# Deformable-convolution block: projections one turn later, one corner instruction, and a product behind every outer product and every addition

## The reference, cut to what matters

```python
# x: (4, 32, 32, 128); G = 8 groups of 16 channels, P = 9 points per pixel and group
xp = gn(x) @ in_w + in_b                          # what is sampled
x1 = silu(batchnorm(depthwise_conv3x3(gn(x))))
offset = x1 @ off_w + off_b                       # (x, y) shift of each point
mask = softmax(x1 @ mask_w + mask_b over the 9 points)
samples = bilinear_sample(xp padded by 1, grid + offset)   # four corners per point
out = (samples * mask).sum(over points) @ out_w + out_b
x = x + out
t = x + attention(layernorm(x));   y = t + experts(layernorm(t))
```

## Time and profile before

| | us |
|---|---|
| median of 3 runs | 665.65 (665.49 to 667.91) |
| the profiled execution's own time | 666.92 |
| its span, first to last instruction | 665.1 |
| PE busy over the span | 599.5 (90%) |
| DVE busy over the span | 550.3 (83%) |
| ACT busy over the span | 234.6 (35%) |
| POOL busy over the span | 320.1 (48%) |

### The profile page before, as it was taken

The page is one execution under the profiler, slowest core; times in us unless marked ns, Lnnn a source line. Parts: engine busy times, 40 slices in busy tenths (PEclk is TensorE's granted clock), DMA queues, the critical chain, the costliest instruction groups (busy, mean ns, idle before and its releaser), DMA issues.

```text
span 665.1 us, 11013 instructions
## 1 busy us (share of the span) xinstructions
PE 599.5 (90%) x3618; PEld 442.4 (67%) x3618; DVE 550.3 (83%) x1030; ACT 234.6 (35%) x351; POOL 320.1 (48%) x408
## 2 busy tenths in 40 slices
PE   5989979979989989889797789999999999979995
PEld 4466656657567667566575567777777777775774
DVE  4668998999999999999999989847767666655877
ACT  6063503405307107126144000344544544415331
POOL 7605775786688578748588810202222211115222
PEclk9789989989989989989997999999999999999999
DMA  7097402103003007000000000000000000004111
GB/s 182 20 337 234 164 0 70 46 3 112 1 3 113 1 1 277 4 1 2 1 1 5 0 1 1 0 2 0 1 1 1 1 1 0 1 6 124 48 33 48
DMA packets 26242, 30.75 MB, mean 46 GB/s; under 512 B 5572, under 2 KB 18324, under 8 KB 26196
## 3 DMA queue, kind: packets, MB, share of 16 engines
q1 hardware_dynamic: 24094, 29.77, 13.8%
q0 software_dynamic: 1408, 0.36, 0.5%
q10 hardware_dynamic: 694, 0.01, 0.1%
HBM read 25.07 MB, written 5.05 MB: 45 GB/s over the span
## 4 chain that ended last, share of the span: by engine, by line
PE 57%; DVE 28%; issue 10%; ACT 2%; DMA 1%; SPq 1%; DVEq 0%; POOL 0%; ACTq 0%; POOLq 0%
DVE prod L1657 13%; PE banks L935 11%; PE banks L1062 9%; PE pair L1042 8%; DVE outer L1589 5%; PE pair L1130 4%; PE banks L1052 4%; PE pair L865 4%; PE banks L1168 4%; PE pair L857 2%; DVE stencil L1598 2%; PE banks L922 2%; PE banks L957 2%; DVE hats L1540 2%; DMA res<-in_x_dram 1%
## 5 line engine op out<-in xcount | busy, mean ns | idle before, releaser
L935 PE MATMUL banks<-ident,prod 128*128 128x128 f32 x1440 | 203.6, 282 | 35.2 <-DVE prod L1657 34.0
L935 PEld LDWEIGHTS banks<-ident,prod 128*128 128x128 f32 x1440 | 165.5, 143 | 91.4 <-DVE prod L1657 64.3
L1657 DVE TENSOR_TENSOR prod<-shifted,stencil 128x1024 f32<-128x1024 f32 (+1 forms) x208 | 218.3, 1084 | 5.2 <-ACT stencil L601 3.5
L1413 POOL TENSOR_TENSOR rstd_now<-mv_now,neg_half 128x2 f32<-128x2 f32 x32 | 22.9, 716 | 124.1 <-DVE mv_now L1705 124.1
L865 PE MATMUL pair<-xg,dw_diag 128*128 128x512 f32 x144 | 74.3, 618 | 1.4 <-DVE xg L1467 1.4
L1308 POOL DMA_INDIRECT got<-padded,cell_now x44 | 57.8, 1314 | 19.0 <-issue 10.1
L1062 PEld LDWEIGHTS banks<-shifted 128*128 128x128 f32 x512 | 60.2, 192 | 8.1 <-issue 6.1
L1062 PE MATMUL banks<-shifted 128*128 128x128 f32 x512 | 63.3, 277 | 2.4 <-ACT shifted L741 1.4
L1589 DVE TENSOR_TENSOR outer<-hats 128x800 f32<-128x800 f32 x56 | 55.8, 996 | 6.1 <-PE banks L922 6.1
L1042 PE MATMUL pair<-shifted 128*128 128x512 f32 x128 | 60.6, 596 | 0.1
L1720 DVE TENSOR_REDUCE neg_max<-pair 128x1 f32<-128x1024 f32 x32 | 39.2, 1225 | 23.1 <-PE pair L1042 22.0
(11 more groups left out here) (264 smaller groups left out, 957.6 us busy)
## 6 DMA issues: line engine op xcount, KB each, us to landing
shifted<-padded SPq DMA_DIRECT2D x42, 256.0 KB
shifted<-padded SPq DMA_DIRECT2D x14, 640.0 KB
res<-in_x_dram SPq DMA_DIRECT2D x4, 512.0 KB, 6.4
padded<-stage SPq DMA_DIRECT2D x4, 512.0 KB, 10.2
stage<-in_L_ffn_W_dram SPq DMA_DIRECT2D x16, 128.0 KB, 2.2
out_dram<-res SPq DMA_DIRECT2D x16, 128.0 KB, 1.8
got<-padded,cell_now POOLq DMA_INDIRECT x44, 2.8
padded<-stencil SPq DMA_DIRECT2D x2, 228.0 KB, 2.6
```

What stands on the lines that cost most here:

```text
L935: mm = pe.matmul(acc_of(c, r), prod[:, slot, r * G:(r + 1) * G, :].rearrange("p g c -> p (g c)"), ident[:, :], is_transpose=True, start=(t ...
L1657: ins = ve.tensor_tensor(prod[:, dx:dx + n, :, :], shifted[:, dx:dx + n, bass.ds(((c % HALF) * ROWS + dy) * G, ROWS * G), :], stencil_of[: ...
```

## The change

Four things are changed together. The products are dealt out differently: one unit between every outer product and its addition, one behind every addition, instead of none or one between and one or two behind. The two corner instructions, of 64 results each, become one of 128 (`outermost` gives the addresses). `project` of chunk k-2 runs in turn k at taps 17, 19, 21, 23, where `project` of chunk k-1 ran at 35 to 41; chunks 5 and 6 are projected between the last chunk's taps, so that only the last chunk is left for the start of the attention. ACT's and DVE's order and waits follow: `residual` moves behind the far counts, `copy_sums` of the last chunk ahead of `residual` of chunk 5, and the last `residual_rest` ahead of the second softmax of the attention.

```diff
-AT_CONV, AT_FAR, AT_OFFSETS, AT_SAMPLES, AT_PROJECT = 4, 15, 30, 31, 35
+AT_CONV, AT_FAR, AT_PROJECT, AT_OFFSETS, AT_SAMPLES = 4, 15, 17, 30, 31
+LAST_PROJECT, LAST_SAMPLES = 8, 20
-POINT_FILL = (1, 0, 1, 0, 1, 0, 1, 0, 0)
-STENCIL_FILL = (0, 2, 1, 2, 1, 2, 1, 2, 2)
+POINT_FILL = (1, 1, 1, 1, 1, 1, 1, 1, 1)
+STENCIL_FILL = (0, 1, 1, 1, 1, 1, 1, 1, 1)
...
+        def outermost(axis, per_column, per_row):
+            first = hats[:, axis, :, :].rearrange("p (g q) t -> p g (q t)", q=PTS)[:, :, 0:1]
+            return bass.AP(tensor=first.tensor, offset=first.offset,
+                           ap=[first.ap[0], first.ap[1], [per_column, 2], [per_row, 2]])
...
                 prepare(j + 2, sums_at=3)
                 clear_stencil(j)
-                if not isinstance(j, int) or j > 0:
-                    residual(j - 1)
                 signs_of(j + 2)
                 if conv_ahead:
                     silu(j + 3)
                 count_out(j + 2)
+                if not isinstance(j, int) or j > 0:
+                    residual(j - 1)
                 copy_out(j)
...
-            residual(CHUNKS - 3)
             copy_sums(CHUNKS - 1)
+            residual(CHUNKS - 3)
             copy_out(CHUNKS - 2)
+            residual(CHUNKS - 2)
             copy_out(CHUNKS - 1)
...
             copy_keys(2)
-            residual_rest(CHUNKS - 2)
             copy_keys(3)
             copy_normed(4)
             exps(0, 0)
+            residual_rest(CHUNKS - 1)
             copy_normed(5)
             copy_keys(4)
             exps(1, 1)
-            residual_rest(CHUNKS - 1)
             copy_keys(5)
...
+                    if t == 0 and c >= 2:
+                        pe.wait_ge(samp_t_done, c - 1)
...
-                    if 0 <= n < B and between == 0 and not first:
-                        project(k - 1, n, n + 1, conv_out if n == B - 1 else None)
+                    if 0 <= n < B and between == 0 and k >= 2:
+                        project(k - 2, n, n + 1, conv_out if n == B - 1 else None)
...
-            add_up(CHUNKS - 1, first_of(BEGIN), AT_SAMPLES)
-            add_fix(CHUNKS - 2)
-            add_up(CHUNKS - 1, AT_SAMPLES, NEAR)
+            for i in range(first_of(BEGIN), NEAR):
+                if i == LAST_SAMPLES:
+                    add_fix(CHUNKS - 2)
+                for k, at in ((CHUNKS - 3, LAST_PROJECT), (CHUNKS - 2, LAST_SAMPLES + 8)):
+                    n, between = divmod(i - at, 2)
+                    if 0 <= n < B and between == 0:
+                        project(k, n, n + 1, conv_out if n == B - 1 else None)
+                add_up(CHUNKS - 1, i, i + 1)
             add_fix(CHUNKS - 1)
-            project(CHUNKS - 2, 0, 1, conv_first)
             project(CHUNKS - 1, 0, 1, conv_first)
...
-            project_rest(CHUNKS - 2, 1)
...
-            project_rest(CHUNKS - 1, 2)
-            project_rest(CHUNKS - 1, 3)
...
-                for kx in range(2):
-                    x0, y0 = (2 * 3 * TAPS + TAPS - 1) * kx, 2 * 3 * TAPS * kx
-                    last = ve.scalar_tensor_tensor(at_corner[:, :, kx, :], at[:, 0, :, x0:x0 + 2 * TAPS + 1:2 * TAPS], 0.0,
-                                                   at[:, 1, :, y0:y0 + 3 * TAPS:2 * TAPS + TAPS - 1], ALU.is_le, ALU.is_lt)
+                last = ve.tensor_tensor(at_corner[:, :, :, :], outermost(0, 2 * 3 * TAPS + TAPS - 1, 2 * TAPS),
+                                        outermost(1, 2 * 3 * TAPS, 2 * TAPS + TAPS - 1), ALU.logical_and)
```

More of the change, by code:

```diff
@@ L707, in _ @@
             copy_sums(CHUNKS - 1)
+            residual(CHUNKS - 3)
             copy_out(CHUNKS - 2)
+            residual(CHUNKS - 2)
             copy_out(CHUNKS - 1)
-            for i, k in enumerate((CHUNKS - 2, CHUNKS - 1)):
-                sc.wait_ge(conv_first, i + 1)
-                residual_of(k, 0, 1)
+            sc.wait_ge(conv_first, 1)
+            residual_of(CHUNKS - 1, 0, 1)
             def copy_normed(j):
@@ L949, in project @@
                 pe.wait_ge(res1_done, CHUNKS - 1 if last else k + 1)
-                if n0 > 0 and done is not None and n1 - n0 > 1:
-                    pe.wait_ge(res1_first, 2 if last else 1)
                 for n in range(n0, n1):
@@ L1081, in attend, with project_rest @@
                     keys(p + LEAD)
-            def project_rest(k, n):
+            def project_rest(n):
                 if n == 1:
-                    pe.wait_ge(res1_first, k - CHUNKS + 3)
-                project(k, n, n + 1, conv_out if n == B - 1 else None)
+                    pe.wait_ge(res1_first, 1)
+                project(CHUNKS - 1, n, n + 1, conv_out if n == B - 1 else None)
             normed_to_t(0)
-            pe.wait_ge(samp_t_done, CHUNKS)
-            project_rest(CHUNKS - 2, 1)
             normed_to_t(1)
             keys(0)
-            project_rest(CHUNKS - 2, 2)
+            project_rest(1)
             normed_to_t(2)
             keys(1)
-            project_rest(CHUNKS - 2, 3)
+            project_rest(2)
             normed_to_t(3)
@@ L1103, in _ @@
             normed_to_t(4)
-            project_rest(CHUNKS - 1, 1)
+            project_rest(3)
             pe.wait_ge(keyed_done, TILES // 2)
@@ L1546, in corners @@
                     ve.sem_inc(dve_waited, 1)
-                at = hats[:, :, :, :].rearrange("p a (g q) t -> p a g (q t)", q=PTS)
-                for kx in range(2):
-                    x0, y0 = (2 * 3 * TAPS + TAPS - 1) * kx, 2 * 3 * TAPS * kx
-                    last = ve.scalar_tensor_tensor(at_corner[:, :, kx, :], at[:, 0, :, x0:x0 + 2 * TAPS + 1:2 * TAPS], 0.0,
-                                                   at[:, 1, :, y0:y0 + 3 * TAPS:2 * TAPS + TAPS - 1], ALU.is_le, ALU.is_lt)
+                last = ve.tensor_tensor(at_corner[:, :, :, :], outermost(0, 2 * 3 * TAPS + TAPS - 1, 2 * TAPS),
+                                        outermost(1, 2 * 3 * TAPS, 2 * TAPS + TAPS - 1), ALU.logical_and)
                 last.then_inc(corners_done, 1)
@@ L1763, in _ @@
                     if j + 1 == TILES // 2 - 1:
-                        ve.wait_ge(res1_first, 2)
+                        ve.wait_ge(res1_first, 1)
+                        ve.wait_ge(res1_done, CHUNKS)
                     token_stats(j + 1, 2 * ((j + 1) % 2), var1)
```

## The result

The changed kernel takes 681.53 us (median of five, 677.95 to 693.01), the kernel before 665.49 us beside it; the ratio is 1.023, interval 1.020 to 1.027. The profiled execution, 693.01 us, is the longest of the five, so the sizes read from it are those of a long one; the kinds of waits are what counts.

A forecast was written before the change was run, and what follows sets the result against it. DVE, 96% busy in turns 0 to 6, was taken to set a turn's length. Terms 7.5 + 2.0 + 0.3 - 1.4 + 1.0 = 9.4 us gave 656.3 us against 665.65, range 653 to 661.2, chance 0.50.

The forecast's parts named there:

- The pauses: On DVE, the 0.11 us between each outer product and its addition goes, 35 times over seven turns, 3.85 us.
- The gaps stay: Rival: DVE still pays the 0.11 us even behind a product; 1.6 us less gain, 657.9 us, chance 0.05.
- the rule on the DRAIN: Skill page: DVE's pipeline empties behind every instruction before the next starts, so the 0.11 us would stay.
- PE's clock no longer falls: Rival: projections fill PE's idle stretch, so its clock stays at 1.00; 2.8 us more gain, 653.5 us, chance 0.18.
- the forecast's terms for turns 0 to 5: Gain 7.5 us: 1.55 a turn in turns 1 to 4, 0.76 in turn 0, about 0.5 in turn 5.
- The new waits for `copy_sums`: DVE, earlier than the chain through PE and ACT, would still wait in turns 1 to 4; 0.61 us in turn 3.
- The first half of a turn: Gaps and corner save 2.6 us; new waits of 0.46 us before outer product 3 cost 2.3; net gain 0.3.
- Turn 6: DVE's wait of 1.70 us before the last chunk goes, plus 0.33 of gaps: gain 2.0 us.
- the last chunk: Eight projections between its taps make DVE's products wait for PE: loss 1.4 us, bounds 0.5 and 6.3.
- the attention: At its start, an earlier residual and two projections fewer in PE's queue bring the scores about 1.0 us earlier.
- the second lump: Last chunk: the later group of four projections over seven taps, said to hold DVE 0.9 us.
- PE has no room: Rival: projections hold outer products 3 to 5 and the last chunk's products; 18.4 us lost, 674.7 us, chance 0.05.

The follow-up runs named there:

- gaps_back: The changed kernel with the two fill tables of before, so the 0.11 us pause between outer product and addition returns: 664.85 us, ratio 0.999.
- no_far_points: The changed kernel with POOL's work on the listed far points left out, the sum staying zero: 652.50 us, ratio 0.981.

## Why the prediction was wrong, point by point

**The step that failed** is the first: "DVE sets the length of a turn, and its idle time and its instruction order are what can be shortened there." For the turns the sum followed DVE, PE and ACT and had no POOL in it, so POOL's chain was put at nothing without a reason, though `add_fix` stands in PE's queue at tap 31 and waits for POOL. No rival spoke of it either. In the changed kernel PE waited there for 35.5 us and DVE's outer products behind it for 41.8; without POOL's work the same kernel takes 652.50 us. The profile of before had two warnings. POOL's lists, in turns of 47.5 us, came 57.5 us apart:
```profile
165.87 0.55 POOL L1386 CAST far_list_i<-far_list 1x8 int32 x1 [2.06 <-issue]
...
223.38 0.95 POOL L1386 CAST far_list_i<-far_list 1x8 int32 x1 [2.21 <-issue]
...
280.89 1.05 POOL L1386 CAST far_list_i<-far_list 1x8 int32 x1 [2.21 <-ACT far_counts L670]
```
and the margin at which PE took its sum shrank from turn to turn: 49.1 us in turn 1, then 29.8, 19.8, and 9.9 in turn 4. There the sum of chunk 3 was done at 277.94 + 0.73 = 278.67, and PE took it at 288.54:
```profile
277.94 0.73 POOL L1353 TENSOR_TENSOR stage<-stage,got_sum 128x16 f32 x1 [0.42 <-POOL got_sum L1351]
```
```profile
288.54 1.06 PE L942 MATMUL banks<-ident,stage 128*128 128x128 f32 x4
```
Two delays of 26.04 and 23.70 us, both ahead of the sum that turn 2 takes, are more than the 29.8 us that it had. And a rule that spoke against this change lay in the section of the Trainium skill just named; I weighed the one on the DRAIN instead.

**The pauses.** That they go was right: in the changed kernel an addition starts at 84.16, where the product ahead ends at 83.03 + 1.21 = 84.24. "The gaps stay" falls, and so the rule on the DRAIN, as the prediction read it, did not hold these additions back. That an unused 0.11 us on DVE costs nothing to take away was wrong: it was POOL's way in.

**The clock.** Without POOL's work the rival "PE's clock no longer falls" came out: the granted clock is 1.00 through turns 0 to 5 against 0.96, and the change gains 11.6 us where the rival gives 9.4 + 2.8 = 12.2. In the changed kernel itself, where PE waits for POOL, it is 0.95 over these turns. That the clock alone makes up the difference from the forecast was not tested. So the forecast's terms for turns 0 to 5, 7.5 us and most of the 0.3, were too small: without POOL they measured 11.8. The new waits for `copy_sums` in turns 1 to 4 did not come either.

**The first half of a turn.** Without POOL's work outer product 3 waited 0.56 us in turns 2 to 5 (forecast 0.46); outer product 2 waits 0.17 to 0.20 as well, which I had not seen. The corner instruction takes 0.34 us, and the next starts 0.26 behind it (forecast 0.24):
```profile
206.95 0.34 DVE L1552 TENSOR_TENSOR at_corner<-hats 128x128 bf16<-128x128 f32 x1 [0.17 <-DVE hats L1545]
207.21 0.98 DVE L1591 TENSOR_TENSOR stencil<-hats 128x800 f32<-128x800 f32 x1
```

**Turn 6, the last chunk, the attention.** Without POOL's work the wait of 1.70 us before the last chunk is gone; that chunk's products show 0.15 + 0.29 + 0.38 = 0.82 us of waits for PE. The forecast was 1.4; by its own terms the second lump holds DVE 0.3 + 2.2 - 1.7 = 0.8 us and not 0.9, so 1.3:
```profile
384.98 11.64 DVE L1659 TENSOR_TENSOR prod<-shifted,stencil 128x1024 f32<-128x1024 f32 x11 [0.15 <-PE banks L942]
396.91 2.96 DVE L1659 TENSOR_TENSOR prod<-shifted,stencil 128x1024 f32<-128x1024 f32 x3 [0.29 <-PE banks L942]
400.26 2.96 DVE L1659 TENSOR_TENSOR prod<-shifted,stencil 128x1024 f32<-128x1024 f32 x3 [0.38 <-PE banks L942]
```
The attention's third maximum comes 18.25 us behind its first statistics, 19.19 without the change: 0.94 us (forecast 1.0).

**The projections.** "PE has no room" falls, with `gaps_back` and with `no_far_points`. That they are worth 0.79 us a turn was not tested by themselves.

## What to carry to other kernels

Before closing pauses on an engine, ask who works in them: an engine with a low busy share (POOL was busy 48% of the span) may live from the pauses of a full one. List every engine's chain with its own period and the margin at which its result is taken, including those that no wait names; a chain whose period is longer than the turn has a margin that shrinks every turn. Where DVE runs two-input instructions beside POOL, keep a pause every few microseconds (here three a turn were enough, together with a later sum) and take POOL's result as late as the queue allows.

## What the runs showed of the hardware that I had not expected

A POOL instruction that elsewhere takes 0.2 to 1.1 us can be held for as long as DVE runs two-input instructions without a pause: 26.04 us over 29 of them, 31.31 in the longest case. A standstill of 0.03 us ends it; a single-input instruction of 0.43 us lets one instruction through, one of 0.20 us none. DVE's own instructions hardly change by it: in the changed kernel outer products take 0.97 us (median) while POOL is held and 0.98 while it works in turns with DVE, then with single ones up to 1.07; while POOL is idle, in `no_far_points`, they take 0.98 as well. Kernels with such long holds spread over 5 to 15 us from one execution to the next (683.38 to 688.47, 686.23 to 701.53), the kernel before over 6.0 (662.66 to 668.67), the version with three pauses and the later sum over 2.2.
